# A front of two batches instead of three, new issue orders on four engines, and VectorE's recurrence written out

## The reference, cut to what matters

```
xn = layernorm(x)
static = xn @ W.T ;  k = q = rmsnorm per head(xn)
o = gated delta rule over the 512 tokens (16 heads of 8x8 state per batch)
y = layernorm(static + o) * w + b
f = w3( gelu( h2( gelu( h1( silu(w1 xn) * (w2 xn) )))))      # width 512
x = x + y + f
xn = layernorm(x)
x = x + linear attention(xn) (16 heads of 8x8, causal, decay per head, no softmax) @ Wo.T + bo
      + xn @ W.T + b + (xn @ V) @ C.T
```

## Time and profile before

| what | before |
|---|---|
| median of 3 runs | 833.37 us (832.61 to 833.41) |
| the profiled execution | 830.45 us, span 828.7 us |
| busy: PE, PEld | 748.3 us (90%), 532.3 us (64%) |
| busy: DVE, ACT, POOL | 739.8 us (89%), 592.1 us (71%), 622.6 us (75%) |
| chain that ended last | PE 61%, POOL 8%, ACT 8%, issue 3%, DVE 1% |
| recurrence (L1210 first, L1229 last end) | 153.1 to 587.7 us |

### The profile page before, as it was taken

One profiled execution on the slowest core, in us unless ns is written; L12 is line 12 of the kernel. 1 busy time (PEld: TensorE's weight loads), 2 busy tenths in 40 slices (PEclk: granted clock), 3 DMA queues, 4 the chain that ended last, 5 costly groups with the idle time before them and its releaser, 6 DMA issues.

```text
span 828.7 us, 12768 instructions
## 1 busy us (share of the span) xinstructions
PE 748.3 (90%) x3433; PEld 532.3 (64%) x3433; DVE 739.8 (89%) x1396; ACT 592.1 (71%) x1363; POOL 622.6 (75%) x623
## 2 busy tenths in 40 slices
PE   4988888388999999999999999998779999999998
PEld 2444443266877887787887788885346656666665
DVE  6889898799999999999999999999688888999887
ACT  7887775668778788778697778778576556666731
POOL 3777778577687777777877766956789778989883
PEclk9999989789999999999999999999799999999999
DMA  6677654600611516125061142060343221211001
GB/s 164 202 254 240 232 182 178 143 14 14 140 38 37 103 38 139 38 56 122 0 133 44 38 99 66 2 180 18 99 127 97 65 64 52 78 52 38 1 27 39
DMA packets 136064, 75.68 MB, mean 91 GB/s; under 512 B 74826, under 2 KB 118860, under 8 KB 136012
## 3 DMA queue, kind: packets, MB, share of 16 engines
q1 hardware_dynamic: 134956, 74.58, 32.5%
q10 hardware_dynamic: 1056, 0.52, 0.2%
HBM read 39.86 MB, written 33.55 MB: 89 GB/s over the span
## 4 chain that ended last, share of the span: by engine, by line
PE 61%; POOL 8%; ACT 8%; issue 3%; DVE 1%; POOLq 0%; ACTq 0%; DVEq 0%
PE f_ps L2204 15%; PE f_ps L2206 10%; PE f_ps L2243 7%; PE f_ps L2334 5%; PE f_ps L2335 5%; PE f_ps L2211 4%; PE f_ps L2311 4%; POOL l_kv L1577 3%; ACT L1823 2%; PE f_ps L2241 2%; PE r_rec L2369 1%; PE r_rec L2363 1%; ACT f_a L1823 1%; ACT f_hh L1838 1%; POOL f_gl L1461 1%
## 5 line engine op out<-in xcount | busy, mean ns | idle before, releaser
L1461 POOL TENSOR_TENSOR f_hl<-f_h,f_hh 128x512 fp32r<-128x512 f32 x64 | 82.4, 1293 | 83.8 <-ACT f_hh L1838 83.8
L1577 POOL TENSOR_TENSOR l_kv<-l_qkv 128x1024 f32<-128x1024 f32 x64 | 124.7, 1952 | 18.8 <-PE f_ps L2335 18.5
L2204 PE MATMUL f_ps<-f_gh,w_hi 128*128 128x512 f32 x256 | 102.8, 402 | 7.6 <-POOL f_gl L1461 7.6
L1216 DVE TENSOR_REDUCE r_rec<-r_pg 128x64 f32<-128x576 f32 x128 | 97.4, 761 | 7.2
L2204 PE MATMUL f_ps<-f_hh,w_hi 128*128 128x512 f32 x256 | 101.4, 396 | 0.4 <-ACT f_b L1827 0.4
L1264 DVE TENSOR_TENSOR l_qs<-f_ps,l_qd 128x1024 f32<-128x1024 f32 x64 | 78.2, 1221 | 22.7 <-PE f_ps L2335 16.1
L1469 POOL TENSOR_TENSOR f_g<-f_a,f_b 128x512 f32<-128x512 f32 x64 | 81.9, 1290 | 16.2 <-ACT f_b L1827 16.2
L1224 DVE TENSOR_REDUCE r_gain<-r_kw 128x128 f32<-128x512 f32 x128 | 87.8, 686 | 4.4
L1461 POOL TENSOR_TENSOR f_gl<-f_g,f_gh 128x512 fp32r<-128x512 f32 x64 | 82.2, 1297 | 3.0 <-ACT f_gh L1833 3.0
L1833 ACT ACTIVATE f_gh<-f_g 128x512 fp32r<-128x512 f32 x64 | 41.1, 642 | 52.1 <-POOL f_g L1469 51.5
L1271 DVE TENSOR_REDUCE l_o_in<-l_qs 128x128 f32<-128x1024 f32 x64 | 77.2, 1211 | 0.6
(11 more groups left out here) (224 smaller groups left out, 2088.2 us busy)
## 6 DMA issues: line engine op xcount, KB each, us to landing
scratch_xnT<-p_xnT SPq DMA_DIRECT2D x16, 256.0 KB, 2.3
scratch_K<-p_kout SPq DMA_DIRECT2D x16, 256.0 KB, 2.3
scratch_fac<-p_fac SPq DMA_DIRECT2D x16, 256.0 KB, 2.0
scratch_R<-p_rr SPq DMA_DIRECT2D x16, 256.0 KB, 3.0
scratch_P<-p_pp SPq DMA_DIRECT2D x16, 256.0 KB, 2.5
first_x<-scratch_xnT SPq DMA_DIRECT2D x16, 256.0 KB, 2.8
first_xt<-in_L_attn_x_dram SPq DMA_DIRECT2D x16, 256.0 KB, 3.0
scratch_W<-r_w SPq DMA_DIRECT2D x16, 256.0 KB, 4.1
```

The lines of the kernel that those rows point to most:

```text
L1216: dve.tensor_reduce(w, pg[q][:, at, :, :, :], AX.X, ALU.add).then_inc(w_ok, 1)
L1461: pool.tensor_tensor(lower, full, upper.bitcast(F32), ALU.subtract).then_inc(done, 1)
L1577: pool.tensor_tensor(dst, k, v, ALU.mult).then_inc(kv_ok, 1)
L2204: nc.tensor.matmul(bank, c.w_hi[:, weights[k], :], upper[k], start=k == 0, stop=False)
```

## The change

The number of front batches goes from 3 to 2; so unit 2 is now the last tiles of batches 0 and 1 (two tiles instead of three), and batch 2 goes through as a whole unit. Step 1, which is `running(0,1)`, joins the set `apart`: it writes the banks of `ps_y` and `ps_x`, and units from FRONT on wait until its scores are read. VectorE's loop is a Python loop, so that its 128 blocks are written out with constant counts. Then the call lists of VectorE, GpSimd, ScalarE, TensorE and SyncE are in a new order from the recurrence's last phases to the end, without the loops over batches. What is computed stays.

```
-    FRONT = 3
+    FRONT = 2
-    apart = {TILES - 5, TILES - 3, TILES - 1}
+    apart = {1, TILES - 5, TILES - 3, TILES - 1}
-        with dve.Fori(0, NSEG // 2) as it:
+        for it in range(NSEG // 2):
...
             reuse(pe, yn_ok, u)
+            if u == FRONT:
+                pe.wait_ge(qs_ok, 2)
...
             reuse(pe, xT_ok, u)
+            if u == FRONT:
+                pe.wait_ge(qs_ok, 2)
...
             if s in apart:
-                pe.wait_ge(yn_ok, B + 1)
-                pe.wait_ge(xT_ok, B + 1)
+                pe.wait_ge(yn_ok, FRONT if s < FRONT else B + 1)
+                pe.wait_ge(xT_ok, FRONT if s < FRONT else B + 1)
...
         project(1, 2)
+        running(0, 1)
         busy()
-        running(0, 1)
+        running(0, 2)
+        outputs(2)
+        running(1, 0)
```

More of the change, by code:

```diff
@@ L1356, in vector @@
         past_state(5, 0)
-        scale2(7)
+        stats2(8)
+        scores(5, 0)
+        block_output(3)
         sums(4, 3)
-        scores(5, 0)
-        sums(5, 0)
+        scale1(10)
         scores(5, 1)
         past_state(5, 1)
-        block_output(4)
[L1364 to L1370, removed]
-        past_state(6, 0)
[L1372 to L1389, removed]
@@ L1698, in gpsimd @@
         outer(6, 3)
[L1699 to L1711, removed]
+        residual(10)
+        outputs(13)
+        decayed(7, 0)
+        outer(7, 0)
+        decayed(7, 1)
@@ L2535, in tensor @@
-        straight(11)
+        queries(4)
+        outputs(10)
+        running(5, 0)
+        normed(7)
+        final(3)
+        past_state(5, 1)
+        project(5, 3)
+        running(5, 1)
+        project(6, 0)
+        attended(4)
+        running(5, 2)
+        straight(4)
+        project(6, 1)
+        past_state(5, 2)
+        running(5, 3)
+        outputs(11)
+        final(4)
+        project(6, 2)
+        running(6, 0)
+        queries(5)
+        normed(8)
+        project(6, 3)
@@ new lines, in tensor @@
+        past_state(6, 0)
+        running(6, 1)
+        project(7, 0)
+        past_state(6, 1)
+        straight(5)
+        running(6, 2)
+        project(7, 1)
+        past_state(6, 2)
+        outputs(12)
+        normed(9)
+        running(6, 3)
+        attended(5)
+        project(7, 2)
+        running(7, 0)
+        final(5)
+        project(7, 3)
+        queries(6)
+        running(7, 1)
+        past_state(7, 0)
+        project(8, 0)
+        straight(6)
+        running(7, 2)
+        project(8, 1)
@@ new lines, in tensor @@
+        attended(6)
+        running(7, 3)
+        past_state(7, 1)
+        normed(10)
+        outputs(13)
+        project(8, 2)
+        running(8, 0)
+        final(6)
+        past_state(7, 2)
+        project(8, 3)
+        queries(7)
+        past_state(8, 0)
+        running(8, 1)
+        attended(7)
+        project(9, 0)
+        past_state(8, 1)
+        running(8, 2)
+        past_state(8, 2)
+        project(9, 1)
+        straight(7)
+        running(8, 3)
+        past_state(9, 0)
@@ new lines, in tensor @@
+        outputs(14)
+        final(7)
+        project(9, 2)
+        running(9, 0)
+        normed(11)
+        past_state(9, 1)
+        project(9, 3)
+        queries(8)
+        running(9, 1)
+        straight(8)
+        past_state(9, 2)
+        project(10, 0)
+        running(9, 2)
+        project(10, 1)
+        attended(8)
+        running(9, 3)
+        project(10, 2)
+        outputs(15)
+        normed(12)
+        past_state(10, 0)
+        running(10, 0)
+        past_state(10, 1)
@@ L2536, in tensor @@
+        project(12, 0)
+        running(11, 2)
+        outputs(16)
+        project(12, 1)
+        attended(10)
+        running(11, 3)
+        final(10)
+        past_state(12, 0)
         project(12, 2)
```

800 lines of the change are left out of this document (471 added, 329 removed).

## The result

The changed kernel took 836.31 us in the median of 18 runs, the kernel before 831.98 us in 18 runs beside it. The ratio of the mean times is 1.0044, with a 95% interval of 1.0031 to 1.0056: slower by 0.44%, where I had forecast 829.9 us and a gain of 3.5. One of the changed kernel's 18 runs took 1471.22 us; it counts in the median but not in the ratio. The profiled execution has a span of 832.5 us (before: 828.7).

What follows compares the result with a forecast made beforehand. TensorE was taken to bound the kernel from 674.3 us, with 8.2 us idle before it recoverable and GpSimd deciding behind the border. Terms 2.6 + 0.9 = 3.5 us took the median from 833.37 to 829.9, range 825.5 to 834.5.

Steps and rivals of the forecast that it cites:

- VectorE's loop: Recurrence: writing out the loop gains 0.5 us of a possible 3.3, since ScalarE's saves pace VectorE; it ends at 587.2.
- TensorE at the border: End of recurrence: running(0,1) ahead of the idle matmuls lets the second scores start at 588.7, 3.9 us earlier.
- GpSimd behind the border: After the recurrence: GpSimd decides, waiting 3.0 us for unit 2's norm; step 5 3.4 us earlier, step 12 only 0.3.
- What TensorE has done by then: Steps 12 to 20: adding TensorE's pieces puts step 20 at 663.8 against 667.31, 2.6 us ahead in work.
- The steady stretch: Second layer's nine later batches: wider gaps between running calls save 0.9 us, 1.5 at best, 0 at worst.
- The sum: Whole kernel: 2.6 + 0.9 = 3.5 us less, span 828.7 to 825.2, median 833.37 to 829.9.
- The rivals: Alternative outcomes: GpSimd eats the gain, 832.5 (0.20); slower, 836.3 (0.16); more, 826.4 (0.14); the loop's whole 3.3 us.
- Slower: GpSimd behind the border: weighted(2), over 3.5 us late for unit 2's norm, gives +2 to +4, 836.3; chance 0.16.

Runs made afterwards that it cites:

- e7: Changed kernel in its column form (e3), with TensorE's running(0, 1) put back behind the three idle matmuls: ratio 1.0004 to the kernel before.
- e3: Changed kernel with VectorE's two small two-SBUF-tensor products done column by column, second operand a per-partition scalar: ratio 0.9963 to the kernel before, median 827.92 us.
- e4: Kernel before the change with VectorE's same two small products done column by column: ratio 0.9977 to the unmodified kernel before.
- e9: Changed kernel with VectorE's scale2 of batch 5 moved two places up, ahead of sums(2, 3) and past_state(3, 0): ratio 1.0086 to the kernel before.
- e10: Changed kernel, VectorE untouched, with two added GpSimd waits for VectorE's small products of batches 5 and 15: ratio 0.9975 to the kernel before.
- e1: Kernel before the change with only VectorE's recurrence loop written out: ratio 1.000 to the unmodified kernel before.

## Why the prediction was wrong, step by step

Times are from the last state update.

- *VectorE's loop*, "I take 0.5": right, 0.7, and for the reason named: three waits for saves instead of one, at phases 18, 22 and 25, where 21, 22 and 25 had been put.
- *TensorE at the border*, "the second scores start at 588.7", 1.5 us behind the recurrence's end: they start about 1.1 behind it, both scores in one piece of 2.35 us. TensorE was ready even 1.7 us sooner than put. Step 1's `running` began 3.3 us ahead of the recurrence's end, where 2.1 was put: the last `project` started 4.7 us ahead of that end, and 3.7 was put. And the clock came back in the middle of it (1.91, then 1.31; a granted clock of 0.72 from 583 to 585 us), so that it took 2.85 us, where I had put 3.4, wholly at half clock. The 3.9 us of earlier scores are worth 3.4 us in the time (e7).
- *GpSimd behind the border*: the wait for unit 2 was 3.06 us against 3.0. Step 5 came at 15.2 us (600.26 less 585.10) against 16.8. Step 12, at 633.62, at 48.5 against 47.7.
- *What TensorE has done by then*, "From 634.9 I add the new order's pieces between the `running` calls": **this is the step that failed.** It takes for granted that TensorE's pieces find their inputs ready. The first that doesn't is `normed(5)`, whose input waited for the held product. Step 13 came 7.70 us behind step 12, with 3.12 us of waiting, where 4.3 had been put (2.6 and 1.72) and e3 takes 4.4; step 20, put at 76.6, came at 81.5 (666.58 less 585.10).
- *The steady stretch*, "0 at worst (other gaps may come up short)": the bound was wrong. The holds at 776 made a hole of 2.25 us and a lower clock behind it, 1.7 us more. The new order's gaps between the `running` calls were in themselves fine: in e3 TensorE is busy for 15.00 us of that window.
- *The sum.* I had put 238.0 us from the recurrence's end (825.2 less 587.2). The column form of the changed kernel takes 238.7, with step 12 at 48.1 and step 20 at 77.6 (47.7 and 76.6 were put). So the account of the queues was right to about 1 us; what it lacked was one resource, worth 8.7 us in the profiles and 6.7 by the ratios. It doesn't follow that the forecast gain of 3.5 us was there behind the holds. The column form gains 1.9 us in the old orders as well (e4), and against e4 the new orders have 1.2 us, which can't be told from none.
- *The rivals.* "Slower" gave 836.3 us, and 836.31 was measured, but that is chance: its mechanism, `weighted(2)` over 3.5 us late, didn't occur (the norm of unit 2 was there 9.2 us behind the recurrence's end; 10.8 had been put). What was to help it, the clock falling behind the idle time before step 5, did occur and cost nothing. None of my cases had VectorE as the engine that is held.

The rows for it were in the trace of before. Its groups by line and shape show VectorE's 128x4 product at a mean of 732 ns and the reciprocal of the same size at 166; the page itself doesn't list so small a group. I read VectorE's rows for their places and not for their durations, and took small instructions to cost nothing.

## What to carry to other kernels

Look for instructions whose mean lies far over that of another of the same size: such a duration can be a wait that no list of waits shows, and a new order can make it longer (1.77 us at most before, 3.95 after) without touching the instruction. Small VectorE instructions on a chain that TensorE waits for should not have two SBUF tensors as operands while GpSimd is kept full; four instructions with a per-partition scalar (0.58 us) were cheaper than one that may be held (0.16 to 5.39 us). A profile is one execution: here the clock fell behind the same idle time in one and not in another, and a comparison of two profiles was off by over 1 us for it. And when an order is judged by adding up queues, the sum should hold what the engines share as well as what each of them does.

## What the runs showed of the hardware

- A VectorE product with two SBUF tensors is held while GpSimd multiplies SBUF tensors: 0.16 us alone, up to 5.39 us beside a full queue (e9), and 0.16 again when GpSimd is made to wait (e10). The column form, one SBUF tensor and a per-partition scalar, wasn't held: 0.20 to 0.22 us in all 116 of e3. Nor was the state update, which has one tensor in PSUM: 0.36 us in all 128 of `after`. GpSimd's own instructions keep their length (0.45 and 1.95 us) meanwhile.
- It was let through at the end of the GpSimd instruction then running in 173 of 178 cases, but not always: in e9 it missed that end after 1.4 us of waiting, and then three more. The hold repeated to 0.01 us between two kernels (3.95 and 3.94). Why some boundaries let it pass and some don't wasn't settled.
- Around step 5 TensorE's clock fell to half in some executions and not in others, for nearly the same idle time before it: before stayed at 1.00 behind 1.53 us and e1 fell to 0.57 behind 1.49 (both from 606 to 610 us). Whether an order makes this more likely wasn't tested.
